# Sorted experts: the expert's bias is added in token order before the sort and travels as the second half of each row

## The reference, cut to what matters

```python
def _L1_ffn_ref(x, Wg, W, b):
    logits = jnp.einsum('bsh,he->bse', x, Wg)
    probs = jax.nn.softmax(logits, axis=-1)
    onehot = jax.nn.one_hot(jnp.argmax(probs, axis=-1), E)
    combine = onehot * probs
    y = jnp.einsum('bsh,ehd->bsed', x, W) + b
    return jnp.einsum('bsed,bse->bsd', y, combine)
...
x = _layernorm(x + _L1_ffn_ref(x, L1_ffn_Wg, L1_ffn_W, L1_ffn_b))
```

## Time and profile before

| | us |
|---|---|
| median of 3 runs | 1118.11 (1111.83 to 1121.18) |
| the profiled execution: its own time | 1117.35 |
| its span, first to last instruction | 1115.6 |
| the last phase, from its first DVE operation to the end | 989.06 to 1115.6 |
| mean granted clock of PE over the span | 0.809 |

### The profile page before, as it was taken

How to read it: one execution, slowest core, us unless ns; L and a number is a source line. 1 busy time by engine, 2 the same in 40 slices (tenths; PEclk the granted TensorE clock), 3 DMA queues, 4 the chain that set the end, 5 groups by cost and what they waited for, 6 DMA issues and landing times. The chain is left out here.

```text
span 1115.6 us, 21541 instructions
## 1 busy us (share of the span) xinstructions
PE 963.5 (86%) x8017; PEld 620.8 (56%) x8017; DVE 603.6 (54%) x2036; ACT 460.2 (41%) x1046; POOL 288.6 (26%) x538
## 2 busy tenths in 40 slices
PE   6866815899779999989998899698999998988995
PEld 3545714777645555548884455343555554854553
DVE  1874793556567777725335444503777772830332
ACT  2563502000026666652226864632566665531222
POOL 1761112455503333310003000000233333323223
PEclk9985559555559999998879998797899999977555
DMA  5145533422200720020000000000000000504000
GB/s 116 29 86 121 192 100 103 87 61 65 56 5 1 210 59 1 1 86 1 1 16 10 1 1 0 1 1 1 1 2 1 1 2 2 190 25 162 25 30 22
DMA packets 51471, 52.28 MB, mean 47 GB/s; under 512 B 8777, under 2 KB 42919, under 8 KB 51112
## 3 DMA queue, kind: packets, MB, share of 16 engines
q1 hardware_dynamic: 41528, 39.59, 13.1%
q10 hardware_dynamic: 7488, 5.53, 2.1%
q0 software_dynamic: 2352, 5.79, 1.6%
HBM read 26.73 MB, written 20.88 MB: 43 GB/s over the span
## 5 line engine op out<-in xcount | busy, mean ns | idle before, releaser
L816 DVE CUSTOM_DVE_ANT_0 l_masked_scores<-psum,mask_q_rows 128x384 bf16<-128x384 f32 (+3 forms) x512 | 225.0, 488 | 76.6 <-PE psum L763 75.7
L838 ACT ACTIVATE l_probs<-psum 128x512 f32<-128x512 f32 (+1 forms) x384 | 186.3, 526 | 150.3 <-PE psum L749 149.6
L851 POOL TENSOR_SCALAR_AFFINE_SELECT l_probs<-l_probs 128x256 f32<-128x256 f32 x256 | 101.5, 409 | 380.0 <-ACT l_probs L838 379.9
L763 PE MATMUL psum<-kb_heads,q_heads 32*128 32x384 f32 (+3 forms) x512 | 109.0, 508 | 10.7 <-DVE l_neg_max_rows L805 8.7
L763 PE MATMUL psum<-l_k_heads,l_q_heads 32*128 32x384 f32 (+3 forms) x512 | 109.4, 509 | 4.6 <-DVE l_neg_max_rows L805 2.7
L749 PE MATMUL psum<-l_q_and_max,l_k_heads 32*128 32x256 f32 (+3 forms) x512 | 112.4, 472 | 0.0
L749 PE MATMUL psum<-l_q_and_max,kb_heads 32*128 32x256 f32 (+3 forms) x512 | 111.9, 470 | 0.0
L781 PE MATMUL psum<-l_probs,rows_32k 128*32 128x512 f32 (+3 forms) x1024 | 97.4, 458 | 2.9 <-POOL l_probs L851 2.9
L749 PEld LDWEIGHTS psum<-l_q_and_max,l_k_heads 32*128 32x128 f32 x512 | 58.9, 188 | 52.1 <-ACT l_probs L838 42.4
L749 PEld LDWEIGHTS psum<-l_q_and_max,kb_heads 32*128 32x128 f32 x512 | 58.6, 187 | 51.7 <-ACT l_probs L838 41.9
L641 POOL TENSOR_TENSOR v_new_and_ones<-v_and_k_rows 32x128 f32<-32x128 f32 x128 | 54.9, 447 | 51.9 <-DVE v_and_k_rows L618 48.3
(11 more groups left out here) (347 smaller groups left out, 1741.5 us busy)
## 6 DMA issues: line engine op xcount, KB each, us to landing
gram_scratch<-rows_32k SPq DMA_DIRECT2D x4, 1024.0 KB, 4.8
rows_32k<-v_new_and_ones SPq DMA_DIRECT2D x64, 64.0 KB, 2.6
sorted_scratch<-l1p_zeros SPq DMA_DIRECT2D x6, 494.5 KB, 8.2
x_rows<-in_L_attn_x_dram SPq DMA_DIRECT2D x16, 128.0 KB, 7.1
heads_scratch<-rows_32k SPq DMA_DIRECT2D x2, 1024.0 KB, 5.4
heads_scratch<-q_kb_T SPq DMA_DIRECT2D x2, 1024.0 KB, 5.7
inverse_scratch<-block_inv SPq DMA_DIRECT2D x2, 1024.0 KB, 4.1
q_heads<-heads_scratch SPq DMA_DIRECT2D x2, 1024.0 KB, 7.1
```

Source lines behind the costliest of these rows:

```text
L763: mm = nc.tensor.matmul(ps[:, row_bank(G, u, i), o:o + w], QT(b, gq)[r, t * P:(t + 1) * P], KT(b, gq)[r, 0:w], start=True, stop=True)
L816: last = nc.vector.tensor_tensor_reduce(out=junk[:, ROW_AT[G, u] % 2, i, o:o + w], in0=ps[:, row_bank(G, u, i), o:o + w], in1=g.maskq[:, N ...
L838: nc.scalar.activation(PT[:, G % 2, 2 * (u % 2) + i, o:o + w], ps[:, e_bank(G, u, i), 0:w], ACT.Exp, scale=SCALE).then_inc(x_ok, 1)
L851: last = nc.gpsimd.affine_select(out=d, in_=d, pattern=[[0, 2], [1, P]], compare_op=ALU.is_ge, fill=0.0, base=0, channel_multiplier=-1)
```

## The change

What it does, edit by edit:

- A row of `XR`, of `sorted_scratch` and of `sorted_rows` becomes `2 * D + 2` = 514 values, 2056 bytes: x, then x + p · b[e], then p and the row's number. Scatters, loads and zeros carry twice the bytes.
- One more DVE step (`cb`, choice times p, 128 × 128) before the slots. PE transposes it, 16 transposes of a 128 × 8 piece; ACT copies the result to SBUF in four pieces; PE multiplies each chunk's 8 × 128 by the 8 × 256 biases, in two PSUM banks; DVE adds each to x and writes the row's second half. POOL's scatter of a chunk waits for that chunk's addition. DVE works out the tiles' experts behind the 16 additions.
- In the loop the bias product is gone, and the expert's product opens the bank itself. DVE's addition and the norm work on the row's second half.
- The 24 products that nobody reads are gone.
- The zeros are written in 23 transfers of 128 × 2056 bytes in place of 6, ahead of the loads of the constants and the expert weights in SP's order; POOL clears its (smaller) tile after its first chunk and not after its fourth.

```diff
@@ phase_out_proj, SP
             sp.dma_start(g.Wg[:, :, :], ...).then_inc(gate_ld, 16)
+            sp.wait_ge(zero_ok, 1)
+            for i in range(NZERO):
+                sp.dma_start(bass.AP(tensor=g.sorted_d.tensor, ..., ap=[[ZW, P], [1, ZW]]), zero[:, :]).then_inc(g.zero_st, 16)
             sp.dma_start(g.route[:, :], g.route_d).then_inc(g.route_ld, 16)
...
-            sp.wait_ge(zero_ok, 1)
-            for i in range(NZERO):
-                sp.dma_start(bass.AP(...), zero[:, :]).then_inc(g.zero_st, 16)
@@ phase_out_proj, POOL
-                if c == 3:
+                if c == 0:
                     nc.gpsimd.memset(zero[:, :], 0.0).then_inc(zero_ok, 1)
@@
-XW = D + 2
+XW = 2 * D + 2
-NZERO = 6
-NFILL = 24
-ZW = NTS * XW // NZERO
+NZERO, ZW = NTS, XW
@@ phase_moe, PE
             pe.wait_ge(gt, 6)
+            pe.wait_ge(g.route_ld, 16)
...
+            pe.wait_ge(gt, 13)
             pe.wait_ge(g.we_ld, 16 * (1 + E))
-            for i in range(NFILL):
-                nc.tensor.matmul(ps[:, 6 + i % 2, :], g.idf[:, :], We[:, i % 2, 0:2, :]..., start=True, stop=True)
-            pe.wait_ge(expert_ok, 2)
+            for q in range(NG):
+                for j in range(G4):
+                    last = nc.tensor.transpose(ps[0:E, 2 + q, j * P:(j + 1) * P], cb[:, q * G4 + j, :], g.idf[:, :])
+                last.then_inc(ct_ps, 1)
+            for c in range(NT):
+                if c % G4 == 0:
+                    pe.wait_ge(ct_sb, c // G4 + 1)
+                if c >= 2:
+                    pe.wait_ge(xb_ok, c - 1)
+                nc.tensor.matmul(ps[:, 6 + c % 2, 0:D], cT[:, c, :], be[:, :], start=True, stop=True).then_inc(b_ps, 1)
+            pe.wait_ge(expert_ok, 1)
...
-                nc.tensor.matmul(ps[:, 4 + t % 2, 0:D], bcast(own[:, t:t + 1], [[0, P]]), be[:, :], start=True, stop=False)
                 pe.wait_ge(t_sb, t + 1)
                 for k in range(KD):
-                    last = nc.tensor.matmul(..., start=False, stop=(k == KD - 1))
+                    last = nc.tensor.matmul(..., start=(k == 0), stop=(k == KD - 1))
@@ phase_moe, ACT
+            for q in range(NG):
+                act.wait_ge(ct_ps, q + 1)
+                nc.scalar.copy(cT[:, q * G4:(q + 1) * G4, :], ps[0:E, 2 + q, :]...).then_inc(ct_sb, 1)
             act.wait_ge(sorted_st, 16 * NT)
...
-                    ln.apply_act(act, s, yo[:, s % 4, :], xs[:, s, 0:D])
+                    ln.apply_act(act, s, yo[:, s % 4, :], xs[:, s, D:2 * D])
@@ phase_moe, POOL
             for c in range(NT):
+                pool.wait_ge(xb_ok, c + 1)
                 nc.gpsimd.indirect_dma_start(out=g.sorted_d, ...)
@@ phase_moe, DVE
-            step(nc.vector.reciprocal(XR[:, :, D], sm[:, :]))
+            step(nc.vector.reciprocal(XR[:, :, 2 * D], sm[:, :]))
+            step(nc.vector.tensor_tensor(cb[:, :, :], oh[:, :, :], bcast(XR[:, 0, 2 * D:2 * D + 1], [[XW, NT], [0, E]]), ALU.mult))
...
             nc.vector.tensor_copy(slot[:, :], pos[:, :]).then_inc(slot_ok, 1)
+            for c in range(NT):
+                dve.wait_ge(b_ps, c + 1)
+                nc.vector.tensor_tensor(XR[:, c, D:2 * D], XR[:, c, 0:D], ps[:, 6 + c % 2, 0:D], ALU.add).then_inc(xb_ok, 1)
             step(nc.vector.tensor_tensor(en[:, :], st[:, :], tl[:, :], ALU.add))
...
-            nc.vector.tensor_scalar(own[:, :], ef[0:E, :], expert_no[0:E, :], None, ALU.is_equal).then_inc(expert_ok, 1)
...
-                    nc.vector.scalar_tensor_tensor(out=xs[:, t, 0:D], in0=ps[:, 4 + t % 2, 0:D], scalar=xs[:, t, D:D + 1], in1=xs[:, t, 0:D], ...)
+                    nc.vector.scalar_tensor_tensor(out=xs[:, t, D:2 * D], in0=ps[:, 4 + t % 2, 0:D], scalar=xs[:, t, 2 * D:2 * D + 1], in1=xs[:, t, D:2 * D], ...)
```

More of the change, by code:

```diff
@@ L2065, in phase_moe @@
         We, be, XR, rt = g.We, g.be, g.XR, g.route
-        lim, below, tile_no, row_no, before, expert_no = (rt[:, ROUTE[i]:ROUTE[i + 1]] for i in range(6))
+        lim, below, tile_no, row_no, before = (rt[:, ROUTE[i]:ROUTE[i + 1]] for i in range(5))
         lg, pr, oh = sb("logits", [P, NT, E]), sb("exps", [P, NT, E]), sb("choice", [P, NT, E])
@@ L2072, in phase_moe @@
         te, expert = sb("tiles_past", [P, NTS, E]), sb("tile_expert", [P, NTS], I32)
-        ef, own = sb("tile_expert_f", [P, NTS]), sb("own_expert", [E, NTS])
+        ef = sb("tile_expert_f", [P, NTS])
+        cb, cT = sb("combine", [P, NT, E]), sb("combineT", [E, NT, P])
+        ct_ps, ct_sb, b_ps, xb_ok = sem("combineT_psum"), sem("combineT_sbuf"), sem("bias_psum"), sem("bias_added")
         order, ones = sb("order", [P, E]), sb("ones", [P, P])
@@ L2104, in _ @@
             nc.tensor.matmul(ps[:, 0, E:NT * E], ones[:, :], run[:, 0, 0:NT - 1, :].rearrange("p c e -> p (c e)"), start=False, stop=True).then_inc(pre_ps, 1)
+            pe.wait_ge(gt, 13)
             pe.wait_ge(g.we_ld, 16 * (1 + E))
-            for i in range(NFILL):
-                nc.tensor.matmul(ps[:, 6 + i % 2, :], g.idf[:, :], We[:, i % 2, 0:2, :].rearrange("p e n -> p (e n)"), start=True, stop=True)
-            pe.wait_ge(expert_ok, 2)
+            for q in range(NG):
[9 more added lines that the diff above has]
+            pe.wait_ge(expert_ok, 1)
             def sortedT(t):
@@ L2123, in product @@
                     pe.wait_ge(u_ok, t - 1)
-                nc.tensor.matmul(ps[:, 4 + t % 2, 0:D], bcast(own[:, t:t + 1], [[0, P]]), be[:, :], start=True, stop=False)
                 pe.wait_ge(t_sb, t + 1)
                 for k in range(KD):
-                    last = nc.tensor.matmul(ps[:, 4 + t % 2, 0:D], xT[:, t % 2, k, :], We[:, k, bass.ds(e, 1), :].rearrange("p e n -> p (e n)"), start=False, stop=(k == KD - 1))
+                    last = nc.tensor.matmul(ps[:, 4 + t % 2, 0:D], xT[:, t % 2, k, :], We[:, k, bass.ds(e, 1), :].rearrange("p e n -> p (e n)"), start=(k == 0), stop=(k == KD - 1))
                 last.then_inc(y_ps, 1)
@@ L2139, in _ @@
             nc.scalar.activation(pr[:, :, :], lg[:, :, :], ACT.Exp).then_inc(ex_ok, 1)
+            for q in range(NG):
+                act.wait_ge(ct_ps, q + 1)
+                nc.scalar.copy(cT[:, q * G4:(q + 1) * G4, :], ps[0:E, 2 + q, :].rearrange("p (c m) -> p c m", c=G4)).then_inc(ct_sb, 1)
             act.wait_ge(sorted_st, 16 * NT)
@@ L2227, in _ @@
                     dve.wait_ge(x_ld[load_of[t]], 16)
-                    nc.vector.tensor_scalar(row[:, t:t + 1], xs[:, t, D + 1:D + 2], -1.0, float(2 * B * N), ALU.mult, ALU.add).then_inc(row_ok, 1)
+                    nc.vector.tensor_scalar(row[:, t:t + 1], xs[:, t, 2 * D + 1:2 * D + 2], -1.0, float(2 * B * N), ALU.mult, ALU.add).then_inc(row_ok, 1)
                     dve.wait_ge(y_ps, t + 1)
-                    nc.vector.scalar_tensor_tensor(out=xs[:, t, 0:D], in0=ps[:, 4 + t % 2, 0:D], scalar=xs[:, t, D:D + 1], in1=xs[:, t, 0:D], op0=ALU.mult, op1=ALU.add).then_inc(u_ok, 1)
+                    nc.vector.scalar_tensor_tensor(out=xs[:, t, D:2 * D], in0=ps[:, 4 + t % 2, 0:D], scalar=xs[:, t, 2 * D:2 * D + 1], in1=xs[:, t, D:2 * D], op0=ALU.mult, op1=ALU.add).then_inc(u_ok, 1)
                 if 3 <= t:
@@ L2234, in _ @@
                     dve.wait_ge(u_ok, t + 1)
-                    ln.stats(dve, t, xs[:, t, 0:D])
+                    ln.stats(dve, t, xs[:, t, D:2 * D])
                 if 3 <= t:
```

8 lines of the change are left out of this document (4 added, 4 removed).

## The result

The changed kernel takes 1079.48 us (median of four runs, 1077.66 to 1083.82) against 1114.97 for the kernel before beside it (four runs, 1111.47 to 1121.18): a ratio of 0.968, with a 95% interval of 0.962 to 0.974. The forecast was 1082, which against the 1118.11 that it started from is a ratio of 0.968. The profiled execution took 1077.66, its span is 1075.9.

What follows compares the result with a forecast made beforehand. PE was taken to bound the loop at half clock, POOL the sort. From the profiled 1117.35, +3.3 + 0.4 + 0.6 = +4.3 and -40.5 for the loop gave 1081.2; the median, 0.8 higher, 1082; range 1073 to 1100.

Steps and rivals of the forecast that it cites:

- pace per tile at full clock: Loop: with the clock risen, 1.75 us per tile, set by the round through the other engines; ends 1.5 and 1.85.
- slow tiles at the start: Loop: two tiles run at 2.44 us each before the clock rises.
- start of the sort: Sort: the first scatter comes 3.3 us later, behind the added step, transposes, bias product and addition.
- last landing: End of the sort: the last scatter's doubled bytes land 0.4 us later.
- first load: Start of the loop: the first tiles' doubled bytes delay it by 0.6 us, bounds 0 to 0.9.
- tail: From the last product's end to the last instruction: 12.1 us, nothing of it changes.
- Rival 1: Loop: the clock stays at the low level, saved 25.8 us, time 1096.7; chance 0.20.
- The round: Loop: product, DVE's addition, ACT's norm and copy, next product: 1.95 + 0.3 + 1.0 = 3.25 us for two tiles.
- Rival 4: Loop: the round stretches to 3.0 us or more per tile, saved 13, time 1109; chance 0.06.
- Rivals 2 and 3: Sort's scatters: POOL writes twice the descriptors, +15.7 us, chance 0.05; or rows are written at half rate, +62, chance 0.03.
- my worst case: Zeros first: SP's issuing lasts to 981, some 8 us more to land, still 4 us of cover before the weights' wait.
- the range stated: Whole time: 1073 to 1100 us, the forecast's own range carried on to rivals 1 and 2.

Runs made afterwards that it cites:

- the second profile: The changed kernel run and profiled once more with no edit: 1074.79 us, ratio 0.965.

## Why the prediction was right

| Term | predicted | measured |
|---|---|---|
| loop, first transpose to last product's end | 42.2, -40.5 | 39.2, -43.5 |
| pace per tile at full clock | 1.75 (1.5 to 1.85) | 1.65 (1.71 from the fifth tile on) |
| slow tiles at the start | 2 | 1 (2 in the second profile) |
| start of the sort | +3.3 | +3.2 (+2.3 in the second profile) |
| last landing | +0.4 | +0.65 |
| first load | +0.6 | +1.0 |
| tail | 0 | -0.3 |
| zeros, 24 idle products, scatters' bytes | 0 | 0 |
| last phase together | -36.2 | -38.9 (-39.3) |

- **The clock.** The step that decided was that the loop's 0.50 comes from its 8-high product and not from too little work. It held, and the two kernels with equal products of 8 and of 128 rows show it directly. Rival 1 fell, in the change and again in the kernel with six transposes per tile; of the rule of the Trainium skill (TensorE: Matmul & The Clock Gate, Part 4: PE-mode transpose) only what the prediction drew from it fell, that transposes in every tile keep the clock low. The evidence in the feed-forward was weaker than I read it, though. The same pairs of a quartet and a 4-high product run at 1.00 from 649.77 to 655.71, with PE busy 5.81 of 5.94 us, right behind the row of 648.82 that I took for a price. And in the kernel before, from 330.60 to 484.20, most of PE's work is products 32 high, several at a time (L749 and L763 start at 399.82, 399.83, 399.83 and 399.84), with PE busy 152.40 of 153.60 us at 1.00. So "low product" alone doesn't say that the clock is low. That it does so in this loop was a bet on the rows that fitted, and the two kernels made it a finding for this loop only.
- **The round.** Its three parts were 1.95, 0.3 and 1.0; they measured 1.96, 0.24 and 1.16. That is 3.36 for two tiles, 1.68 each, and not 1.63, because DVE starts 1.16 behind the product's start and not 1.0. I had rounded 1.63 up to 1.75 for fear of gaps. There are hardly any: the 18 tiles from the fifth on took 1.71 each, 0.7 us less than I gave them together. That the rounding came close is partly luck, since it covered the part that I had too short. Rival 4 had nothing to it.
- **The first tiles** were the term I mis-sized. The first four intervals from product to product took 6.03 us where I had 8.38 (twice 2.44 and twice 1.75). In the second profile the clock rose after two slow tiles, as forecast, and the four still took 6.57. So most of the error is not the rise: the slow tiles take 2.1 to 2.3 and not 2.44, and the tiles right after them 1.1 to 1.6 before the round closes. The 2.35 and the 0.7 are the 3 us by which the loop beat the forecast.
- **The sort.** +3.3 was right as a sum. In its parts the transposes took 3.6 where I had 3.5 at half speed (3.2 in the second profile), the addition 0.42, and the bias products came every 0.9 and not every 1.15, which changed nothing since POOL is the pace. Rivals 2 and 3 fell with the scatters at 0.97 and 1.28 apart; the wide rows alone cost 1.8 us, where landing and load had 1.0 in the sum.
- **The zeros.** SP issued them from 942.68 on in 14.4 us and was through with all at 967.2, well before the 981 of my worst case; nothing waited for the weights.
- **The range.** 1075 to 1088 for the forecast's own ends is narrower than these ends added up (1074 to 1090). It made no difference to the range stated.
- **What I didn't price.** The projection's 4.8 us in the profiled run. It was outweighed there by phases further ahead, whose code is the same and which came out 5.6 us shorter: the sum for the last phase (-38.9), the projection (+4.8) and these (-5.6) is the -39.7 between the two profiled executions. The median's near miss, 2.5 us, is smaller than such differences, so that it is this small is luck and no proof of the terms. The last phase is the proof, and there the forecast was 2.7 to 3.1 us short.

## What to carry to other kernels

A product with few rows in every turn of a loop of full-height ones can cost far more than its own time: here 1.15 us of 3.59 went and 1.9 came off every tile, because the granted clock doubled. Look for the odd low product wherever the profile shows PE busy and the clock at half. It is a suspect and no more, since products 4 and 32 high stand at 1.00 elsewhere in this trace; the test is one run with the product made 128 high in place. Then make it high, or move it to a place that isn't PE's bound; what it cost to move it here was 4 us of 43. When PE has become fast, read the round through the other engines before doing more to PE, and start such a loop with the clock up, with no more idle products than fit ahead of the first load.

## What the runs showed of the hardware that I had not expected

- PE busy 82.58 us of 82.60 with one 8-high product per tile: clock 0.50. PE busy 28.35 of 35.90 with none: clock 1.00. PE busy 40.34 of 40.60 with a 128-high one in its place: 0.93, and 1.00 from 5.8 us on.
- The clock's rise comes at different distances from the loop's first instruction: 3.2 and 5.6 us in two profiles of one kernel, 6.3 in a like one.
- Products 32 high, several at a time, kept PE busy 152.40 of 153.60 us at a clock of 1.00; products 16 high (L443) kept it busy 20.00 of 20.00 us at 0.50.
- A DVE operation on one value per partition took 3.29 us instead of 0.15 beside gapless POOL additions and a DMA share of 1.07, in 3 of 14 profiles; with the fall of the clock that followed, 4.9 us. Another profile has the same additions and DMA share without it.
- With the norm five tiles back, DVE's additions began up to 2.3 us and ACT's copies up to 3.1 us after everything that they wait for had ended by the records; in the twelve other profiles this is 0.04 us throughout the loop.
- An indirect scatter of 128 rows takes POOL 0.97 us with 1032 bytes a row and with 2056.
